# Keys turned on VectorE and by DMA, first states and the last block copies moved to ScalarE, in a gated delta rule layer with experts

## Chip, cores and metric

The kernel runs on one core of a Trainium2 chip, in one launch. The metric is device microseconds for the launch; lower is better. TensorE is called PE below, VectorE DVE, ScalarE ACT, GpSimd POOL and SyncE SP.

## What is computed

All tensors are float32, with 2 sequences of 512 tokens of width 256. The output is `x + delta_rule(xn) + ffn(xn)`, where `xn` is the layernorm of `x`. The second branch is attention with 16 heads, a shared expert and 16 routed experts with 4 picks per token. The first branch has 16 key heads and 32 value heads (R = 2 per key head), and takes most of the second half of the time:

```python
for each chunk:                      # the reference has chunks of 64 tokens, the kernel 128
    T  = solve(I + tril(beta * K K^T * decay, -1))     # T is the inverse
    vn = T @ (V * beta) - (T @ (K * beta * exp(g))) @ state
    out   = (Q * exp(g)) @ state + tril(Q K^T * decay) @ vn
    state = state * exp(g_last) + (K * exp(g_last - g))^T @ vn
x = out * silu(z); x = x * rsqrt(mean(x * x) + eps) * norm_weight
y += x @ W_out                       # per head
```

## The kernel before

Every engine has its own instruction stream, written out by hand in one function; semaphores (`fl["..."]`) are all that joins them. The order on an engine is the order of the calls in the code.

After the attention and the experts comes the part that the change touches: `for h in range(NK)` with NK = 16, on every engine. In pass h the scan of head h runs (two sequences b, four chunks m of 128 tokens), while head n = h + 1 is prepared (gates, values, triangular solve) and head f = h + 2 is begun (keys, queries, decays). PSUM is one tensor `ps` of 8 banks; X and Y are bank pairs 4, 5 and 6, 7.

What the text speaks of:

- PE's scan steps: `solved(h, m, b)` (L857) multiplies by the inverse PT; ACT's `deltas(h, m, b)` (L1440) takes the result to `vs`; `new_state(h, m, b)` (L867) multiplies the decayed, turned keys WT with it and waits for the deltas (`a_d`); `chunk_output` (L889, L890) follows; `key_state` (L843) multiplies the keys with the state; DVE's `residuals` (L2003) subtracts.
- DVE's `states(h, m, b)` (L2016 for m = 0, a copy; L2022 else) writes the state `St` from PSUM.
- `turn_keys(n)` (L797) transposes the 8 key tiles of head n on PE into the pair Y, and ACT's `decayed_keys(n, r)` (L1458) scales them into WT, 8 instructions for each r. It stands between `solved(h, 1, ·)` and `new_state(h, 1, ·)`.
- `project_gates` (L835) is filler between scan steps; PE's first one of a head waits for DVE's `system(n, ·)` (L1988), which writes MT and needs the decays that POOL's `scaled_decays` (L2373) finishes. `attention(n, r)` (L1996) writes AT.
- The inverse is built by doubling. `beside_64` and `blocks_of_128` are the last two steps; each takes two PSUM banks to SBUF, the first bank on ACT (L1503, L1507), the second on DVE (L2135, L2139).
- SP issues the DMAs: MT's diagonal blocks of 32 to DRAM (L392) and to `MTc` (L397, printed as front), back into `blk` (L404), then the decays of head f (L336). `T64c` holds turned blocks of the inverse.
- `add_experts(i)` (L2094) adds gathered expert rows: four instructions in each of the passes 0 to 7.

Of the kernel before, what the change touches and what calls it, by code (L numbers as in the profile page):

```python
# [45 lines left out]
def build(nc, d, out, debug=None):  # L46
# [9 lines left out]
    with ExitStack() as ctx:  # L56
# [200 lines left out]

        def stage_bank(f, i):
            return ((2, 0), (2, X))[f][i] if f < 2 else (X, Y)[i]
# [7 lines left out]
        def tiles(bank):  # L267
# [13 lines left out]
            "p_kq", "p_v", "p_z", "p_ss", "p_kk", "p_kt", "p_qk", "p_vt", "p_ks", "p_tr", "p_w", "p_o", "p_sx", "p_wo",  # L281
# [3 lines left out]
            "v_ck", "v_cv", "v_ss", "v_k2", "v_cb", "v_M", "v_A", "v_R", "v_S", "v_g", "v_sxt", "v_sx", "v_add",  # L285
            "v_base", "v_t0", "v_tt", "v_u3", "v_p3", "v_vs", "v_self",
# [13 lines left out]
        def _(sp):  # L300
# [86 lines left out]
            def blocks_out(n):  # L387

                sp.wait_ge(fl["v_M"], 2 * n + 2)
                for q in range(4):  # L390
                    rows = slice(q * BL, (q + 1) * BL)
                    dma(mt_dram[q].rearrange("u p c -> p u c"), MT[rows, :, rows]).then_inc(fl["d_m"], 16)  # L392
                if n:
# [75 lines left out]
            for s in range(SLOTS + 4):  # L469
# [6 lines left out]
                if s == SOLVE - 3:  # L476
                    blocks_in(0)
                if s == SOLVE + SB + 4:
# [44 lines left out]
        def _(pe):  # L523
# [268 lines left out]
            def turn_keys(n):  # L792
# [5 lines left out]
                last.then_inc(fl["p_kt"], 1)  # L798

            def project_values(n, r):  # L800
# [7 lines left out]
                elif r == 0:  # L808
                    pe.wait_ge(fl["a_wk"], 2 * n + 2)
# [30 lines left out]
            def key_state(h, m, b):  # L840

                pe.wait_ge(fl["v_S"], 6 * h + 2 * (m - 1) + b + 1)
# [3 lines left out]
            def solved(h, m, b):  # L846
# [3 lines left out]
                else:  # L850
# [3 lines left out]
                    pe.wait_ge(fl["a_p3"], h + 1)  # L854
                    pe.wait_ge(fl["v_p3"], h + 1)
# [169 lines left out]
            def second_beside_64_and_first_of_128(n):  # L1025

                pe.wait_ge(fl["a_u3"], n + 1)
# [9 lines left out]
            def second_of_128(n):  # L1037

                pe.wait_ge(fl["v_u3"], n + 1)
# [118 lines left out]
            for h in range(NK):  # L1158
# [28 lines left out]
                if middle:  # L1187
                    turn_keys(n)
# [77 lines left out]
        def _(act):  # L1266
# [170 lines left out]

            def deltas(h, m, b):
# [12 lines left out]
            def decayed_keys(n, r):  # L1451
                if r == 0:
                    act.wait_ge(fl["p_kt"], n + 1)
                    act.wait_ge(fl["v_cb"], n + 1)
                    if n >= 2:
                        act.wait_ge(fl["p_w"], 6 * (n - 1))
                for t in range(NT):
                    last = fn(WT[:, n % 2, r, t, :], tiles(Y)[:, t, :], ACT.Copy, scale=cb[:, r, 1, t:t + 1])  # L1458
# [42 lines left out]
            def beside_64(n):  # L1501
# [1058 lines left out]
```

## Time and profile before

| | |
|---|---|
| median of 3 runs | 1564.86 us (1560.41 to 1567.17) |
| profiled execution, its own time | 1548.47 us |
| its span, first to last instruction | 1546.7 us |
| granted TensorE clock, mean | 0.998 |
| PE / DVE / ACT / POOL busy | 98% / 71% / 50% / 29% |

The share of busy time is that of the whole span. Busy time of a run of matmuls on PE counts each until its modelled end, so the distance from one start to the next says what it costs.

### The profile page before, as it was taken

How to read it: one execution, taken by the hardware profiler on the slowest of the kernel's cores; microseconds unless marked ns; L12 is line 12 of the kernel's file. 1: busy time of each engine (PE TensorE's matmuls, PEld its weight loads, DVE VectorE, ACT ScalarE, POOL GpSimd, SP SyncE). 2: the span in 40 equal slices, each digit the busy share in tenths (PEclk: the TensorE clock that was granted, in tenths of full speed). 3: DMA queues.
4: the chain of work that ended last, by engine and by line, in shares of the span. 5: the costliest groups of instructions: out<-in, count | busy, mean ns of one | idle time of the engine just before them, and what ended most of it. 6: DMA issues, size and time to landing. Idle time of an engine off the chain costs nothing.

```text
span 1546.7 us, 29212 instructions
## 1 busy us (share of the span) xinstructions
PE 1514.5 (98%) x10946; PEld 1069.7 (69%) x10946; DVE 1104.5 (71%) x2452; ACT 779.7 (50%) x1680; POOL 442.7 (29%) x280
## 2 busy tenths in 40 slices
PE   6999999999999999999999999999999999999998
PEld 4666666767656776666767767767767668668667
DVE  5364544465366335698988988988888988988966
ACT  3444445344423334664564664664664565565552
POOL 1000000006024003354444444543442541541511
PEclk9999999999999999999999999999999999999999
DMA  4342433223144434324314414414313323223211
GB/s 135 99 150 96 156 124 109 66 64 125 54 128 130 124 109 120 94 51 97 100 35 107 107 32 108 105 36 106 78 50 91 70 60 86 69 66 86 60 22 35
DMA packets 225051, 136.88 MB, mean 89 GB/s; under 512 B 160976, under 2 KB 196304, under 8 KB 224912
## 3 DMA queue, kind: packets, MB, share of 16 engines
q1 hardware_dynamic: 221840, 126.62, 30.5%
q0 software_dynamic: 3072, 8.39, 1.8%
q8 instruction: 89, 1.46, 0.4%
q14 instruction: 50, 0.41, 0.1%
HBM read 94.85 MB, written 35.91 MB: 85 GB/s over the span
## 4 chain that ended last, share of the span: by engine, by line
PE 90%; DVE 3%; issue 2%; POOL 2%; ACT 1%; DMA 1%; SPq 0%; POOLq 0%; DVEq 0%; ACTq 0%
PE ps L953 7%; PE ps L814 7%; PE ps L575 7%; PE ps L835 6%; PE ps L670 5%; PE ps L600 4%; PE ps L1089 4%; PE ps L704 4%; PE ps L857 3%; PE ps L590 3%; PE ps L890 3%; PE ps L742 3%; PE ps L752 3%; PE ps L1112 3%; PE ps L867 3%; PE ps L889 2%
## 5 line engine op out<-in xcount | busy, mean ns | idle before, releaser
L1440 ACT ACTIVATE vs<-ps 128x256 f32<-128x256 f32 x128 | 49.2, 384 | 255.8 <-PE ps L857 251.6
L2389 POOL TENSOR_TENSOR qg<-qT,Ebc 128x1024 f32<-128x1024 f32 x32 | 74.7, 2354 | 354.4 <-PE ps L890 329.2
L1944 DVE SCALAR_TENSOR_TENSOR cv<-ps,cw,cv 128x1022 f32<-128x1022 f32 (+2 forms) x96 | 122.8, 1280 | 18.9 <-ACT cv L1380 14.9
L1955 DVE SCALAR_TENSOR_TENSOR cv<-ps,cw,cv 128x1022 f32<-128x1022 f32 (+2 forms) x96 | 122.6, 1277 | 4.0 <-ACT cv L1412 1.6
L835 PE MATMUL ps<-xnT,gz 128*128 128x512 f32 x256 | 121.0, 596 | 0.6 <-DVE cv L1944 0.6
L953 PE MATMUL ps<-wout,xT 128*128 128x256 f32 x480 | 120.2, 392 | 1.3 <-ACT vs L1427 0.9
L575 PE MATMUL ps<-xrT,cv 128*128 128x512 f32 x256 | 117.8, 593 | 1.1 <-ACT xrT L1277 0.8
L814 PE MATMUL ps<-xnT,gv 128*128 128x512 f32 x256 | 117.6, 603 | 0.5
L2083 DVE SCALAR_TENSOR_TENSOR total<-ps,rr,total 128x256 f32<-128x256 f32 x240 | 111.6, 481 | 5.7
L1340 ACT ACTIVATE we<-ps,bias 128x128 f32<-128x128 f32 (+3 forms) x128 | 65.8, 526 | 98.2 <-DVE bias L1764 98.2
L1760 DVE TENSOR_TENSOR ps<-ps,causal_neg 128x128 f32<-128x128 f32 x128 | 37.4, 292 | 105.2 <-PE ps L600 105.2
L953 PEld LDWEIGHTS ps<-wout,xT 128*128 128x128 f32 x480 | 86.1, 189 | 24.9 <-issue 11.7
L2373 POOL TENSOR_TENSOR dec<-dec,cb 128x1024 f32<-128x1024 f32 x32 | 60.0, 1897 | 147.5 <-DVE cb L1977 134.4
L814 PEld LDWEIGHTS ps<-xnT,gv 128*128 128x128 f32 x256 | 46.1, 189 | 71.0 <-issue 57.9
L890 PE MATMUL ps<-AT,vs 128*128 128x128 f32 x512 | 91.1, 275 | 0.0
L857 PEld LDWEIGHTS ps<-vs,PT 128*128 128x128 f32 x512 | 65.9, 191 | 24.1 <-issue 14.2
L2339 POOL TENSOR_SCALAR mean<-ssq 128x4 f32<-128x4 f32 x2 | 0.4, 192 | 284.9 <-ACT junk L1324 284.9
L1380 ACT ACTIVATE cv<-ps,cw 128x1024 f32<-128x1024 f32 x32 | 35.7, 1115 | 87.6 <-PE ps L752 61.1
L2359 POOL TENSOR_TENSOR dec<-dec,e_neg 128x1024 f32<-128x1024 f32 x32 | 75.2, 2373 | 0.0
L600 PE MATMUL ps<-front,we 128*128 128x128 f32 (+3 forms) x256 | 74.2, 433 | 0.8 <-ACT front L1283 0.8
L575 PEld LDWEIGHTS ps<-xrT,cv 128*128 128x128 f32 x256 | 46.1, 190 | 41.4 <-issue 39.4
L889 PE MATMUL ps<-qg,St 128*128 128x128 f32 x384 | 74.4, 275 | 0.0
(265 smaller groups left out, 3567.9 us busy)
## 6 DMA issues: line engine op xcount, KB each, us to landing
xs_dram<-zeros SPq DMA_DIRECT2D x16, 1024.0 KB, 7.6
dec<-grow_dram SPq DMA_DIRECT2D x32, 512.0 KB, 4.7
Ebc<-erow_dram SPq DMA_DIRECT2D x32, 512.0 KB, 5.0
cv<-in_wqk SPq DMA_DIRECT2D x16, 512.0 KB, 3.6
xn<-xs_dram SPq DMA_DIRECT2D x47, 128.0 KB, 2.1
ys_dram<-yg SPq DMA_DIRECT2D x47, 128.0 KB, 2.0
we<-in_we SPq DMA_DIRECT2D x16, 352.0 KB
cv<-in_wv SPq DMA_DIRECT2D x16, 256.0 KB, 3.7
```

Of the source, the lines that this page charges most:

```text
L575: last = mm(ps[:, 6 + j % 2, :], wqk[:, i, c, w * P:(w + 1) * P], xrT[:, c, at:at + S], start=(c == 0), stop=(c == HK - 1))
L600: mm(score(i, qt), aqT[:, q:q + P], akT[:, i * S:i * S + (qt + 1) * P], start=True, stop=True).then_inc(sm["s_sc"], 1)
L670: last = mm(ps[:, 6 + i, kt * P:S], vt[:, kt, i * P:(i + 1) * P], probT[:, 4 * i + kt, kt * P:S], start=(kt == 0), stop=(kt == 3), skip_gr ...
L814: last = mm(ps[:, (Y, X)[r] + b, :], gv[:, k, r * D:(r + 1) * D], xnT[:, k, b * S:(b + 1) * S], start=(k == 0), stop=(k == HK - 1))
L835: last = mm(ps[:, gate_bank(n) + b, :], gz[:, k, r * D:(r + 1) * D], xnT[:, k, b * S:(b + 1) * S], start=(k == 0), stop=(k == HK - 1))
L857: last = mm(ps[:, b, r * D:(r + 1) * D], PT[:, r * NT + 4 * b + m, :], vs[:, r, 4 * b + m, :], start=True, stop=True)
L889: mm(dst, St[:, m % 2, b * R + r, :], qg[:, r, t, :], start=True, stop=False)
L890: last = mm(dst, vs[:, r, t, :], AT[:, h % 2, r, t, :], start=(m == 0), stop=True)
L953: last = mm(ps[:, output_bank(h, t), r * H:(r + 1) * H], xT[:, r, t * P:(t + 1) * P], wout[:, r, :], start=True, stop=True)
L1944: ins = stt(row, pair(bank)[:, :, 0:S - k], cw[:, f, i, TAPS - 1 - k:TAPS - k], row, ALU.mult, ALU.add)
L1955: ins = stt(row, pair(bank)[:, :, 0:S - k], cw[:, n, 2 + r, TAPS - 1 - k:TAPS - k], row, ALU.mult, ALU.add)
L2083: ins = stt(total[:, t, :], ps[:, output_bank(h, t), r * H:(r + 1) * H], rr2[:, r, t:t + 1], total[:, t, :], ALU.mult, ALU.add)
```

## The change

- PE turns only head 0's keys. For n from 1 on DVE's new `turn_keys(n)` transposes the 32 x 32 blocks of all 8 tiles in one instruction (128 x 1024) from kT into T64c, and SP's new `keys_across(n)` carries the 16 blocks of the 4 x 4 grid to their places in WT, in 16 DMAs. ACT's `decayed_keys` scales from WT to WT, both after `gate_silu(n, 1)`.
- T64c loses its zeros by this, so POOL's new `empty_side(n)` clears a quarter of its rows and half of their columns when the DMAs have landed.
- DVE's copies of the first states go to ACT's `first_states`, and DVE's halves of the last two doubling steps go to ACT too.
- `add_experts(i, half)` adds two rows' tiles in each of the 16 passes, and the gathers are issued every second pass.
- SP issues the blocks back in before `MTc`, the keys behind them, and the decays of head f last.

```diff
+        turned_keys = T64c[:].rearrange("p u c -> p (u c)").rearrange("p (t n) -> p t n", t=NT)
+        def copies(n):
+            return 64 + (64 + 256) * n
@@ SP
+            def keys_across(n):
+                if n >= 2:
+                    sp.wait_ge(fl["p_w"], 6 * (n - 1))
+                sp.wait_ge(fl["x_kt"], n + 1)
+                for i in range(4):
+                    for j in range(4):
+                        src = turned_keys[i * BL:(i + 1) * BL, :, j * BL:(j + 1) * BL]
+                        dma(WT[j * BL:(j + 1) * BL, n % 2, 0, :, i * BL:(i + 1) * BL], src).then_inc(fl["d_c"], 16)
...
                     blocks_in(n)
+                    blocks_across(n)
+                    keys_across(n)
@@ PE
                     if f >= 2:
-                        pe.wait_ge(fl["a_wk"], 2 * f)
+                        pe.wait_ge(fl["v_A"], 2 * f)
...
-                pe.wait_ge(fl["d_c"], 64 * (n + 1))
+                pe.wait_ge(fl["d_c"], copies(n))
...
                         solved(h, 1, b)
-                if middle:
-                    turn_keys(n)
@@ ACT
+            def first_states(h, b):
+                act.wait_ge(fl["p_w"], 6 * h + b + 1)
+                if h:
+                    act.wait_ge(fl["p_o"], 8 * h)
+                fn(St[:, 1, b * R:(b + 1) * R, :].rearrange("p r d -> p (r d)"), ps[:, b, R * D:],
+                   ACT.Copy).then_inc(fl["x_S"], 1)
...
-            beside_64(0)
+            beside_64(0, 0)
+            beside_64(0, 1)
             gate_silu(0, 1)
             decays(1, 0)
             decays(1, 1)
-            blocks_of_128(0)
+            blocks_of_128(0, 0)
+            blocks_of_128(0, 1)
@@ DVE
+            def turn_keys(n):
+                dve.wait_ge(fl["p_u3"], 2 * n)
+                dve.transpose(turned_keys.rearrange("p t n -> p (t n)"), kT[:, n % 2].rearrange("p t n -> p (t n)"))                   .then_inc(fl["x_kt"], 1)
...
-                    for r in range(R):
-                        attention(n, r)
+                    attention(n, 0)
+                if middle:
+                    turn_keys(n)
                 if scan:
                     for b in range(B):
-                        states(h, 0, b)
+                        residuals(h, 1, b)
+                if middle:
+                    attention(n, 1)
@@ POOL
+            def empty_side(n):
+                pool.wait_ge(fl["d_c"], copies(n))
+                pool.memset(T64c[0:BL, :, BL:2 * BL], 0.0).then_inc(fl["g_zero"], 1)
```

PE's instructions from pass 0's second chunk, before (L857 `solved`, L797 `turn_keys`, L867 `new_state`, L889 `chunk_output`):

```order
L857 MATMUL ps<-vs,PT 128x128 [waits v_R]
L857 MATMUL ps<-vs,PT 128x128
L797 MATMUL ps<-ident,kT 128x128 [waits v_A]
L797 MATMUL ps<-ident,kT 128x128 x7
L867 MATMUL ps<-vs,WT 128x128 [waits a_d]
L867 MATMUL ps<-vs,WT 128x128
```

and of the changed kernel (L877 and L887 are `solved` and `new_state` there):

```order
L877 MATMUL ps<-vs,PT 128x128 [waits v_R]
L877 MATMUL ps<-vs,PT 128x128
L887 MATMUL ps<-vs,WT 128x128 [waits a_d]
L887 MATMUL ps<-vs,WT 128x128
L887 MATMUL ps<-vs,WT 128x128 [waits a_d]
```

Nothing stands any more between the product and the one that waits for its deltas.

SP's issues in pass 0, before:

```order
L392 DMA mt_dram<-MT 32x16x32 x3
L397 DMA front<-MT 32x16x32 [waits p_u1]
L397 DMA front<-MT 32x16x32 x3
L404 DMA front<-mt_dram 64x16x16 [waits d_m]
L404 DMA front<-mt_dram 64x16x16
L336 DMA dec<-grow_dram 128x1024 [waits v_A]
```

and of the changed kernel (L422 is `blocks_in`, L405 `blocks_across`, L415 `keys_across`):

```order
L422 DMA front<-mt_dram 64x16x16 [waits d_m]
L422 DMA front<-mt_dram 64x16x16
L405 DMA front<-MT 32x16x32 [waits p_u1]
L405 DMA front<-MT 32x16x32 x3
L415 DMA WT<-T64c 32x8x32 [waits x_kt]
L415 DMA WT<-T64c 32x8x32 x15
L341 DMA dec<-grow_dram 128x1024 [waits v_A]
```

Sixteen issues came in ahead of the decays, behind two sets that changed places.

ACT ahead of the loop, before (`beside_64`, `gate_silu(0, 1)`, `decays(1, ·)`, `blocks_of_128`):

```order
L1503 ACTIVATE U3s<-ps 64x512 [waits p_u3]
L1465 ACTIVATE sz<-ps 128x1024 [waits p_z]
L1469 ACT_TABLE_LOAD
L1469 ACTIVATE dec<-dec 128x1024 [waits g_mask] x2
L1507 ACTIVATE PT<-ps 64x8x64 [waits p_p3]
```

and of the changed kernel:

```order
L1531 ACTIVATE U3s<-ps 64x512 [waits p_u3] x2
L1493 ACTIVATE sz<-ps 128x1024 [waits p_z]
L1497 ACT_TABLE_LOAD
L1497 ACTIVATE dec<-dec 128x1024 [waits g_mask] x2
L1536 ACTIVATE PT<-ps 64x8x64 [waits p_p3] x2
```

The second of the two U3s copies waits for PE's second set of products there, and the decays of head 1 stand behind it.

## Rows read from the trace of the kernel before

**Rows 1.** Page, part 1: busy us (share of the span), instructions.

```profile
PE 1514.5 (98%) x10946; PEld 1069.7 (69%) x10946; DVE 1104.5 (71%) x2452; ACT 779.7 (50%) x1680; POOL 442.7 (29%) x280
```

**Rows 2.** Windows, two passes: length, busy of PE, PEld, DVE, ACT, POOL, PEclk, DMA.

```profile
706.25:765.21 58.96, 58.92 (x535) 42.28 (x534) 52.19 (x108) 33.87 (x64) 26.44 (x16) 1.00 0.34 81
1355.17:1414.12 58.95, 58.91 (x534) 42.27 (x533) 50.61 (x104) 33.86 (x64) 22.52 (x12) 1.00 0.32 74
```

**Rows 3.** Timeline of PE in one pass: start us, us, engine, line, operation.

```profile
941.32 1.05 PE L857 MATMUL ps<-vs,PT 128*128 128x128 f32 x8
942.21 1.04 PE L797 MATMUL ps<-ident,kT 128*128 128x128 f32 x8
943.09 1.06 PE L867 MATMUL ps<-vs,WT 128*128 128x128 f32 x8
...
958.83 0.38 PE L889 MATMUL ps<-qg,St 128*128 128x128 f32 x2
```

**Rows 4.** Timeline of PE in the last pass, which has no fillers.

```profile
1517.05 1.10 PE L857 MATMUL ps<-vs,PT 128*128 128x128 f32 x8
1518.17 1.16 PE L867 MATMUL ps<-vs,WT 128*128 128x128 f32 x8
1519.17 1.06 PE L890 MATMUL ps<-AT,vs 128*128 128x128 f32 x8
...
1521.36 1.23 PE L857 MATMUL ps<-vs,PT 128*128 128x128 f32 x8 [0.27 <-DVE vs L2003]
1522.54 1.23 PE L867 MATMUL ps<-vs,WT 128*128 128x128 f32 x8
1523.61 0.39 PE L889 MATMUL ps<-qg,St 128*128 128x128 f32 x2
```

**Rows 5.** Timeline of ACT in that pass; in brackets idle time before.

```profile
949.72 2.17 ACT L1458 ACTIVATE WT<-ps,cb 128x128 f32<-128x128 f32 x8
...
952.76 1.08 ACT L1465 ACTIVATE sz<-ps 128x1024 f32<-128x1024 f32 x1
956.86 0.83 ACT L1440 ACTIVATE vs<-ps 128x256 f32<-128x256 f32 x2 [3.02 <-PE ps L857]
```

**Rows 6.** Timeline of DVE in that pass.

```profile
933.81 1.21 DVE L1988 TENSOR_TENSOR MT<-ps,dec 128x1024 f32<-128x1024 f32 x1
...
938.11 0.75 DVE L2016 COPY St<-ps 128x256 f32<-128x256 f32 x2
```

**Rows 7.** Groups of DVE by form: busy, mean ns, idle before.

```profile
L2040 DVE STREAM_TRANSPOSE front<-ps 128x512 f32<-128x512 f32 x15 | 10.8, 717 | 1.5
```

**Rows 8.** Timeline of SP in that pass.

```profile
935.05 2.04 SPq L392 DMA_DIRECT2D mt_dram<-MT  x4
```

**Rows 9.** Two lines of SP: ns min/median/max of an issue, first and last start.

```profile
L397 SPq DMA_DIRECT2D front<-MT x64: 617/634/1827, 500.0 to 1469.9; - x64
...
DMA to landing us min/median/max: 2.2/2.4/4.0
```

**Rows 10.** The same for the 64 loads of 16 x 16 x 16.

```profile
L418 SPq DMA_DIRECT2D front<-tbt_dram x64: 303/448/474, 565.1 to 1495.0; - x64
```

**Rows 11.** Timeline ahead of the loop: PE, then ACT.

```profile
632.80 0.22 PE L1007 MATMUL ps<-T64c,MT 64*64 64x64 f32 x1
...
630.14 0.59 ACT L1503 ACTIVATE U3s<-ps 64x512 f32<-64x512 f32 x1
630.76 1.02 ACT L1465 ACTIVATE sz<-ps 128x1024 f32<-128x1024 f32 x1
...
633.09 2.00 ACT L1469 ACTIVATE dec<-dec 128x1024 f32<-128x1024 f32 x2
```

**Rows 12.** Timeline of pass 0: POOL, then DVE, then PE.

```profile
634.29 3.75 POOL L2373 TENSOR_TENSOR dec<-dec,cb 128x1024 f32<-128x1024 f32 x2 [13.11 <-ACT dec L1469]
...
638.08 1.23 DVE L1988 TENSOR_TENSOR MT<-ps,dec 128x1024 f32<-128x1024 f32 x1
...
639.71 1.88 PE L835 MATMUL ps<-xnT,gz 128*128 128x512 f32 x4
```

More of the change, by code:

```diff
@@ L477, in _ @@
                     blocks_in(0)
+                    blocks_across(0)
                 if s == SOLVE + SB + 4:
@@ L797, in turn_keys @@
                     last = pe.transpose(tiles(Y)[:, t, :], kT[:, n % 2, t, :], ident[:])
-                last.then_inc(fl["p_kt"], 1)
+                last.then_inc(fl["x_kt"], 1)
             def project_values(n, r):
@@ L1451, in decayed_keys @@
             def decayed_keys(n, r):
[L1452 to L1456, printed above, removed]
+                if n == 0:
+                    act.wait_ge(fl["x_kt"], 1)
+                else:
+                    act.wait_ge(fl["d_c"], copies(n))
+                act.wait_ge(fl["v_cb"], n + 1)
+                if n >= 2:
+                    act.wait_ge(fl["p_w"], 6 * (n - 1))
                 for t in range(NT):
-                    last = fn(WT[:, n % 2, r, t, :], tiles(Y)[:, t, :], ACT.Copy, scale=cb[:, r, 1, t:t + 1])
+                    src = WT[:, n % 2, 0, t, :] if n else tiles(Y)[:, t, :]
+                    last = fn(WT[:, n % 2, r, t, :], src, ACT.Copy, scale=cb[:, r, 1, t:t + 1])
                 last.then_inc(fl["a_wk"], 1)
@@ L1499, in blocks_of_64, with beside_64, blocks_of_128 @@
                    ACT.Copy).then_inc(fl["a_p2"], 1)
-            def beside_64(n):
-                act.wait_ge(fl["p_u3"], 2 * n + 1)
-                fn(U3s[64:P, 0:8], ps[64:P, 0, :].rearrange("p (u c) -> p u c", u=8), ACT.Copy).then_inc(fl["a_u3"], 1)
-            def blocks_of_128(n):
-                act.wait_ge(fl["p_p3"], 2 * n + 1)
-                fn(PT[0:64, 0:8, 64:P], ps[0:64, 0, :].rearrange("p (u c) -> p u c", u=8),
+            def beside_64(n, a):
+                act.wait_ge(fl["p_u3"], 2 * n + a + 1)
+                fn(U3s[64:P, 8 * a:8 * a + 8], ps[64:P, a, :].rearrange("p (u c) -> p u c", u=8),
+                   ACT.Copy).then_inc(fl["a_u3"], 1)
+            def blocks_of_128(n, a):
+                act.wait_ge(fl["p_p3"], 2 * n + a + 1)
+                fn(PT[0:64, 8 * a:8 * a + 8, 64:P], ps[0:64, a, :].rearrange("p (u c) -> p u c", u=8),
                    ACT.Copy).then_inc(fl["a_p3"], 1)
@@ L1589, in _ @@
                     for b in range(B):
+                        first_states(h, b)
+                    for b in range(B):
                         deltas(h, 1, b)
@@ L1596, in _ @@
                         deltas(h, 2, b)
-                if middle:
-                    decayed_keys(n, 1)
                 if scan:
@@ L1609, in _ @@
                     take_key(f, 0)
+                if ahead:
                     silu_key(f)
@@ L1645, in _ @@
                 if middle:
-                    beside_64(n)
+                    beside_64(n, 0)
                 if middle and not ahead:
@@ L1651, in _ @@
                 if middle:
-                    blocks_of_128(n)
+                    beside_64(n, 1)
+                    blocks_of_128(n, 0)
+                    blocks_of_128(n, 1)
         @block.vector
@@ L2087, in add_outputs, with add_experts @@
                     ins.then_inc(fl["v_add"], 1)
-            def add_experts(i):
-                for a in range(4):
+            def add_experts(i, half):
+                for a in range(2 * half, 2 * half + 2):
                     t, j = i % 2 * 4 + a, i // 2
@@ L2225, in _ @@
             second_values(0)
-            beside_64(0)
             for h in range(NK):
@@ L2233, in _ @@
                     system(n, 0)
-                if scan and middle:
-                    blocks_of_128(h)
                 if middle:
@@ L2240, in _ @@
                 if middle:
-                    for r in range(R):
-                        attention(n, r)
-                if scan:
-                    for b in range(B):
-                        states(h, 0, b)
+                    attention(n, 0)
+                if middle:
+                    turn_keys(n)
                 if scan:
@@ L2297, in _ @@
                     add_outputs(h, 4, 5)
-                    beside_64(n)
                     add_outputs(h, 5, 7)
@@ L2462, in _ @@
                 if middle:
+                    empty_side(n)
+                if middle:
                     if not ahead:
@@ L2476, in _ @@
                     key_norms(f)
-                if 0 <= n < 8:
-                    expert_rows(n)
+                if h % 2 and n // 2 < 8:
+                    expert_rows(n // 2)
 _OUT = (2, 512, 256)
```

58 lines of the change are left out of this document (23 added, 35 removed).

## The prediction

> **What bounds the kernel now.** I read the page's first part, then the windows of single passes, then the timelines of PE, ACT, DVE and SP around the places that the change touches. PE is busy 98% of the span [rows 1]. The windows run from the key turn of one pass to that of the next: 58.96 and 58.95 us, with PE busy 58.92 and 58.91 in them, while DVE has 52.19 and 50.61 and ACT 33.9 [rows 2]. The reader is to see two passes 650 us apart that have the same length to a hundredth: each pass costs exactly what PE has to issue, and nobody makes PE wait. Only 0.04 us are left. So what counts is what leaves PE's stream, and which wait comes up in its place. DVE has 6.8 us or more idle in a pass; relief for DVE is worth nothing by itself, and the 0.75 us for two state copies [rows 6] don't go to the time.
>
> **What is removed from PE.** The eight transposes start at 942.21 and the next group at 943.09 [rows 3], so they cost 0.88 us of PE's issue. They go in 15 passes (n = 1 to 15; head 0 stays): 13.2 us. I take the distance of starts and not the 1.04 us of the row, which reaches into the next group.
>
> **The wait that comes up.** The transposes covered something. `new_state(h, 1, 0)` needs ACT's deltas of `solved(h, 1, 0)`, and with the transposes gone both sequences' solves are all that stands between. The trace has this case: in the last pass no filler is left, and the solve is followed at once by the new state. Solve and new state together take 0.89 + 0.89 us when they don't wait (941.32 to 942.21 is one of them [rows 3]). In the last pass they take 1519.17 - 1517.05 = 2.12 us for m = 0 and 1523.61 - 1521.36 = 2.25 us for m = 1 [rows 4], so the pause is 0.34 or 0.47 us. In the second one the solve itself was still waiting for DVE's residuals; in the passes of the loop those lie under a filler, so the first is the nearer row and I take 0.34. What is left of the gain is 0.88 - 0.34 = 0.54 us a pass, times 15 = 8.1 us. Bounds: 0.41 x 15 = 6.2 us, and 13.2 us if ACT were quick enough for no pause at all, for which no row speaks.
>
> **What the ACT change costs ahead of the loop.** This is the part that I would overlook from the diff. `beside_64(0, 1)` stands ahead of `gate_silu(0, 1)` and the two decays of head 1 on ACT, and it waits for PE's second set of products. Those are issued until 632.80 + 0.22 = 633.0, while ACT's own first copy was done at 630.73 and the gate began at 630.76 [rows 11]. Now: second copy 633.1 to 633.7 (0.59), gate to 634.7 (1.02), table load to 636.0 (the 1.3 us between 631.78 and 633.09), so the decays start at 636.0 in place of 633.09, 2.9 us later. POOL's scaling followed the first of them: 634.29 becomes 637.2, and its two instructions (3.75 us) end at 641.0. DVE's second `system` starts right behind (638.08 before), takes about 1.15 us and ends at 642.2. PE's first gates of the pass started at 639.71 [rows 12] and wait for it: 2.5 us lost, once. PE then has nothing that gives them back, since it is the bound. Below, the cost is 2 us if parts overlap better; above, 3.5 us, since POOL's row gathers and the expert rows behind them come as much later as well, and `states(0, 1)` is queued behind those on DVE. Inside the loop the same move costs nothing: ACT's second U3s copy and the two PT copies lie under `key_products`, and DVE's copies did so before.
>
> **The keys' way round.** DVE: one transpose of 128 x 1024. The nearest rows are 0.717 us for 128 x 512 [rows 7] and 1.21 us for an operation of 128 x 1024 [rows 6]; 1.2 us, in a place from which two state copies (0.75) and one block copy went. DVE stays ahead of PE, cost 0. SP: `system(n, 1)` ended at 935.0 and SP began at 935.05 [rows 6, 8]; it is now about 1.2 us earlier, as two copies of the size of ACT's 0.59 us [rows 11] are gone from DVE ahead of it. From 933.85: 2.04 us for four issues [rows 8], some 1.7 for their landing (2.4 less an issue of 0.63 [rows 9]), two issues and then four at 0.63 with small gaps, 1.3 + 2.7: the keys' first issue is at 941.6. Sixteen issues follow. An issue took 0.634 us for 32 x 16 x 32 from SBUF to SBUF [rows 9] and 0.448 for 16 x 16 x 16, which is as many pieces as 32 x 8 x 32 has [rows 10]. So 7.2 to 10.1 us, and the last lands 1.8 us later: 950.6 to 953.5; I take 0.5 an issue, 951.4. ACT: the key scalings (2.17 us each [rows 5]) now both stand behind the second gate. It started at 952.76 with one scaling ahead of it; without that it waits for PE's gate products only and ends near 951.8. Then 4.3 us of scaling to 956.1, and `deltas(h, 3, ·)`, which began at 956.86 [rows 5], now 956.3 with PE ahead by 0.54. PE asks for the first of them at 958.83 - 0.54 = 958.3 [rows 3], and one takes 0.45: ACT may be 1.5 to 1.7 us late before PE loses anything, that is, the keys may land at 953.5. Even the upper bound just fits. Cost 0, with a cliff right behind it. If the cover is gone, every us of landing costs PE a us in 14 or 15 passes.
>
> The Trainium skill speaks against this part (VectorE: DVE Perf Modes, The three transpose paths): a plain DMA that transposes by strides is 19 times slower than the crossbar's transpose, which it puts at 1309 ns for 128 x 128 in bf16, and a full 128 x 128 turn belongs on TensorE. An estimate from that page would be 25 us a tile, and the keys would never be in time. Here DVE turns inside the blocks, and a DMA moves whole rows of 32 numbers; the four block transfers of MT are of that kind and land in 2.4 us [rows 9], so the sum goes by them.
>
> **Other edits at nothing.** The first states go from DVE to ACT, where ACT sat idle before the next deltas; DVE began at 938.11, ACT can begin with the products and be done before `key_state`. The split `add_experts` moves 2 of 4 additions from the early passes to the late ones, both with idle DVE. POOL's clearing lies in a wait for PE. `project_keys` waits for AT in place of WT, which is done sooner. `dec` is asked for some 10 us later on SP, and POOL uses it only behind the queries of the pass.
>
> **Sum.** -8.1 + 2.5 + 0.3 for small things in pass 0 = -5.3 us. The profiled execution took 1548.47 us (span 1546.7 and 1.8 around it), so it would become 1543.2. The median of the runs shown is 1564.86, 1.1% above that execution; I carry the difference over unchanged: 1559.5 us, 0.34% less. What a measurement of this kernel can tell from no change is about 0.5%, or 7.8 us.
>
> **Rivals.**
>
> - *The forecast*: PE stays the bound, a pass is 0.54 us shorter (58.41 us), 2.5 to 3 us lost at the start. 1557 to 1562. Chance 0.62.
> - *The gain stays nearly whole*: the pause after the solve is 0.1 to 0.2 us, or the start costs little, since POOL's and DVE's parts overlap. 15 x 0.73 - 2.5 = 8.5 us: 1556, and 1552 at the very best (13.2). For it: ACT is idle ahead of these deltas. Against it: ACT was idle in the last pass too, and the pause was there [rows 4]. Chance 0.19.
> - *The keys land late, and the time goes up*: one mechanism, SP's sixteen issues in a row. If an issue costs 0.70 in place of 0.5 us (L397 has single issues of 1.8 [rows 9]), they land at 954.6, 1.1 us past the point where ACT's deltas hold PE up; 14 passes x 1.1 = 15 us against 5.3 gained: 1575. It decides for slower than before from 0.655 us an issue on (0.38 us a pass). For it: no row has a DMA with both sides strided in SBUF, and no row has 26 issues in a run. Against it: the median of the larger transfer is 0.634. The page's rule on strided copies would end here too, far beyond. Chance 0.15.
> - *The change does nothing*: pause 0.47, start 3.5 us, ACT late in the last but one pass (it has no key projections between the fourth solve and its outputs, so the margin of 1.5 us is not there, about 1 us once): 6.2 - 3.5 - 1 = 1.7 us gained, 1563. Chance 0.04; it lies inside the range.
>
> **Range and chances.** From the middle of the second case to where the third has just begun: 1554 to 1569. Faster by over 0.5% needs over 7.8 us, the second case: 0.19. Slower by over 0.5% needs the third with 0.94 us a pass and more, most of it: 0.14. Within 0.5%: 0.67.
>
> **What would show it.** In the windows a pass of 58.4 us with PE busy some 0.3 less than that, and DVE still with idle time. In PE's timeline the new-state group (L887) starts 1.1 to 1.2 us after the solve for m = 1, with a wait for ACT. Ahead of the loop PE's first gates of pass 0 wait 2.5 us for DVE. On SP sixteen issues of 0.45 to 0.6 us, and ACT's scaling without a wait for DMA. The prediction is wrong if ACT waits for the keys until past 953.5 in the clock of rows 5 and PE then waits for ACT ahead of the outputs of m = 3, or if the pause after the solve is not there.

## The result and the profile after

The changed kernel takes 1592.36 us (median of 4 runs, 1584.41 to 1600.95), and the kernel before, measured beside it, 1562.63 us (4 runs, 1557.25 to 1567.17). The ratio is 1.019, 95% interval 1.012 to 1.0265: slower, outside the predicted range, on the side of the third rival. The profiled execution took 1597.63 us, span 1595.8.

The page of the changed kernel, part 1, for [rows 1]:

```profile
PE 1519.4 (95%) x10826; PEld 1065.4 (67%) x10826; DVE 1098.1 (69%) x2403; ACT 816.6 (51%) x1744; POOL 450.5 (28%) x295
```

PE's share fell from 98% to 95%: it has 120 instructions less and yet a longer span. Windows of four passes, from `key_products` (now L801) to the next, with the columns of [rows 2]:

```profile
650.22:717.56 67.34, 61.58 (x524) 43.65 (x524) 47.82 (x97) 39.57 (x70) 28.87 (x19) 0.95 0.31 67
717.56:777.74 60.18, 58.32 (x528) 41.33 (x524) 50.65 (x104) 36.18 (x67) 23.05 (x15) 1.00 0.35 80
1143.02:1203.61 60.59, 58.43 (x528) 41.24 (x525) 50.68 (x104) 36.17 (x67) 26.96 (x19) 1.00 0.38 88
1203.61:1263.60 59.99, 58.33 (x529) 41.33 (x525) 50.65 (x104) 36.19 (x67) 23.04 (x15) 1.00 0.35 80
```

A pass is no longer the same each time (59.2 to 67.3 us, against 58.95 to 59.5), and 1.7 to 2.2 us lie between its length and PE's busy time (5.8 in the first pass), where there was 0.04. So PE waits. The view of waits, largest sum us, times, longest us, says for what:

```profile
ACT WT L1486 <- DMA WT<-T64c: 51.1, 15, 4.8
...
PE ps L909 <- ACT vs L1465: 28.2, 15, 5.4
```

L1486 is ACT's `decayed_keys`, L1465 its `deltas`, L909 PE's `chunk_output`. Once in each of 15 passes ACT waits for the keys' DMAs, and once PE waits for ACT. The pass at 1143.02 shows how the one makes the other. SP's timeline, for [rows 8]:

```profile
1147.49 2.06 SPq L397 DMA_DIRECT2D mt_dram<-MT  x4
1152.18 1.35 SPq L422 DMA_DIRECT2D front<-mt_dram  x2
1153.57 2.69 SPq L405 DMA_DIRECT2D front<-MT  x4
1156.36 11.28 SPq L415 DMA_DIRECT2D WT<-T64c  x16
```

Then the timelines of ACT and PE in the same stretch, for [rows 5] and [rows 3]:

```profile
1162.13 0.83 ACT L1465 ACTIVATE vs<-ps 128x256 f32<-128x256 f32 x2 [3.28 <-PE ps L877]
...
1164.30 1.02 ACT L1493 ACTIVATE sz<-ps 128x1024 f32<-128x1024 f32 x1 [0.30 <-PE ps L856]
1168.94 4.78 ACT L1486 ACTIVATE WT<-WT,cb 128x128 f32<-128x128 f32 x16 [3.62 <-DMA WT<-T64c]
1173.63 0.63 ACT L1465 ACTIVATE vs<-ps 128x256 f32<-128x256 f32 x2
...
1169.36 1.05 PE L877 MATMUL ps<-vs,PT 128*128 128x128 f32 x8
1170.25 1.88 PE L763 MATMUL ps<-xnT,gkq 128*128 128x512 f32 x4
1174.05 0.49 PE L909 MATMUL ps<-qg,St 128*128 128x128 f32 x2 [1.91 <-ACT vs L1465]
```

The sixteen issues take 11.28 us and the last one lands with the start of ACT's scaling at 1168.94. ACT runs in order: the deltas of m = 3, whose products PE had done by 1170.4, stand behind the scaling, the first of them ends at 1174.0, and PE, which has worked off all its fillers by 1172.1, waits 1.91 us. The line of the keys' DMAs by itself (ns min/median/max of an issue; us to landing):

```profile
L415 SPq DMA_DIRECT2D WT<-T64c x240: 585/611/1848, 667.8 to 1528.9; - x120
...
DMA to landing us min/median/max: 1.9/2.0/3.3
```

**Where the time went.** From the first `key_products` of the loop to its last one, which is passes 0 to 13, the changed kernel needs 853.95 us and the kernel before 826.3: +27.65. The last two passes and what follows take 91.66 and 86.45: +5.2, with a wait of 5.44 us at the same place. Together 32.9 us, against a difference of the medians of 29.7. The profiled execution is longer still, since its loop starts at 650.22 and not at 633.90. That is not the change: those 16.3 us arise in the first stage, whose code is the same. There DVE stood still for 7 us in front of a copy while POOL issued its scatters of rows (`xs_dram`), and then took 9.36 us for four small operations (1.27 us in the profile before), beside two of POOL's (371.54 to 376.2):

```profile
369.00 0.69 DVE L1777 COPY front<-ps 128x512 f32<-128x512 f32 x1 [7.05 <-issue]
...
371.21 9.36 DVE L1933 TENSOR_SCALAR we<-we,prec 128x128 f32<-128x128 f32 x4
```

The loop starts at 632.9 to 633.9 in the profiles of e4 and e7 to e16, which have the same first stage, and at 641 to 651 in those of e1, e3, e5 and e6; e5 has the first stage of the kernel before, and its loop starts at 646.8. The kernel before, measured beside each of them, took 1561.98 us beside e1, e3, e5 and e6 and 1548.89 to 1551.01 beside the others. So times are compared by their ratio to it, and everything else below is read from the loop.

### The profile page after: what moved, and what is told of

Its sections match the earlier page's. It is cut to its first block, busy times and chain, and to the rows that moved or that the text cites. A ratio compares the mean times of both kernels' runs of the same rounds, so it can differ in the third digit from the quotient of the medians.

```text
span 1595.8 us, 29241 instructions
## 1 busy us (share of the span) xinstructions
PE 1519.4 (95%) x10826; PEld 1065.4 (67%) x10826; DVE 1098.1 (69%) x2403; ACT 816.6 (51%) x1744; POOL 450.5 (28%) x295
## 4 chain that ended last, share of the span: by engine, by line
PE 67%; SPq 12%; DVE 8%; ACT 6%; issue 3%; DMA 3%; POOL 0%; another core or an unknown queue 0%; POOLq 0%; ACTq 0%; DVEq 0%
SPq L415 9%; PE ps L973 7%; PE ps L596 7%; ACT WT L1486 4%; PE ps L691 4%; PE ps L835 4%; PE ps L621 4%; DVE cv L1979 4%; PE ps L1109 4%; PE ps L725 3%; PE ps L773 3%; PE ps L611 3%; PE ps L1132 3%; PE ps L679 2%; PE ps L1027 2%
## 5 line engine op out<-in xcount | busy, mean ns | idle before, releaser
L835 PE MATMUL ps<-xnT,gv 128*128 128x512 f32 x256 | 117.9, 604 | 3.3 <-DVE cv L1979 3.3
L1465 ACT ACTIVATE vs<-ps 128x256 f32<-128x256 f32 x128 | 47.0, 379 | 140.9 <-PE ps L877 134.2
L909 PE MATMUL ps<-qg,St 128*128 128x128 f32 x384 | 79.3, 290 | 28.3 <-ACT vs L1465 28.2
L1486 ACT ACTIVATE WT<-WT,cb 128x128 f32<-128x128 f32 x240 | 71.7, 388 | 51.1 <-DMA WT<-T64c 51.1
L910 PE MATMUL ps<-AT,vs 128*128 128x128 f32 x512 | 94.8, 283 | 0.0
L835 PEld LDWEIGHTS ps<-xnT,gv 128*128 128x128 f32 x256 | 46.8, 191 | 71.0 <-issue 54.9
L909 PEld LDWEIGHTS ps<-qg,St 128*128 128x128 f32 x384 | 61.2, 201 | 40.2 <-ACT vs L1465 40.2
L2043 DVE SCALAR_TENSOR_TENSOR vs<-ps,gates,vs 128x128 f32<-128x128 f32 x192 | 54.2, 345 | 44.1 <-PE ps L864 42.8
L2405 POOL MEMSET T64c<- 32x512 f32 x15 | 7.7, 514 | 264.7 <-DMA WT<-T64c 264.7
L877 PEld LDWEIGHTS ps<-vs,PT 128*128 128x128 f32 x512 | 65.9, 191 | 23.8 <-issue 14.2
```

The source lines that it names most:

```text
L835: last = mm(ps[:, (Y, X)[r] + b, :], gv[:, k, r * D:(r + 1) * D], xnT[:, k, b * S:(b + 1) * S], start=(k == 0), stop=(k == HK - 1))
L909: mm(dst, St[:, m % 2, b * R + r, :], qg[:, r, t, :], start=True, stop=False)
L910: last = mm(dst, vs[:, r, t, :], AT[:, h % 2, r, t, :], start=(m == 0), stop=True)
L1486: last = fn(WT[:, n % 2, r, t, :], src, ACT.Copy, scale=cb[:, r, 1, t:t + 1])
```

## The experiments

The theory: SP's issue time makes the keys late, and ACT's order carries the lateness to PE. The first rival: ACT is overloaded by what was moved to it, whenever the keys come.

**e3: four DMAs in place of sixteen.** They carry the same bytes, but whole rows, so that WT doesn't hold the turned keys.

```diff
-                    for j in range(4):
-                        src = turned_keys[i * BL:(i + 1) * BL, :, j * BL:(j + 1) * BL]
-                        dma(WT[j * BL:(j + 1) * BL, n % 2, 0, :, i * BL:(i + 1) * BL], src)
+                    for j in (i,):
+                        src = turned_keys[i * BL:(i + 1) * BL]
+                        dma(WT[j * BL:(j + 1) * BL, n % 2, 0], src)
```

> The changed kernel, but the turned blocks go to WT in 4 DMAs of 32 x 8 x 128 in place of 16 of 32 x 8 x 32: the same bytes, a quarter of the issues, and the blocks off the diagonal don't change places, so WT is not the transpose. Theory (SP's sixteen issues in a row make the keys late, and ACT's deltas of the fourth chunk are queued behind them): the keys land some 7 us earlier, ACT's wait for them (51 us in total in the changed kernel) falls under 2 us, PE's wait ahead of the fourth chunk's outputs (28 us) under 3 us, the granted clock no longer dips in the loop, a pass is 58.5 to 58.7 us, and the whole takes about 30 us less than the changed kernel, some 3 us less than the one before. Rival (ACT itself has too much between the second gate and those deltas since the first states, block copies and both scalings are there): PE still waits 1 us or more a pass, less than 15 us are won.

Measured 1552.98 us, ratio 0.9945 (0.9924 to 0.9966). SP's part in one pass:

```profile
1133.48 2.49 SPq L415 DMA_DIRECT2D WT<-T64c  x4
```

The passes are 61.12 and then 58.30 to 58.41 us, and the wait ahead of L909 is gone up to the last pass but one, where 0.94 us are left. ACT does all it does in the changed kernel, so it isn't overloaded.

**e1: ACT's scaling behind the deltas.**

```diff
                     gate_silu(n, 1)
-                    decayed_keys(n, 1)
-                    decayed_keys(n, 0)
...
                         deltas(h, 3, b)
...
                     take_key(f, 1)
+                    decayed_keys(n, 1)
+                    decayed_keys(n, 0)
                     take_key(f, 0)
```

> The changed kernel with all 16 DMAs, but ACT scales the keys behind the fourth deltas and the take of head f's keys. Theory (the landing hurts only because ACT takes its queue in order): PE's wait ahead of the fourth outputs is gone, a pass is 58.4 to 58.7 us, the whole about 3 us below the kernel before. Rival (ACT overloaded): the wait shows up again at the convolutions, PE's projection of the values waits for DVE by 0.5 us a pass or more, and a pass stays above 59 us.

Measured 1561.43 us, ratio 0.9997 (0.9977 to 1.0017). The keys come as late as ever and PE doesn't wait for deltas any more; behind the first pass they take 58.75 to 58.87 us. ACT in one of them:

```profile
1142.84 0.83 ACT L1465 ACTIVATE vs<-ps 128x256 f32<-128x256 f32 x2 [4.68 <-PE ps L877]
1145.01 1.11 ACT L1398 ACTIVATE cv<-ps,cw 128x1024 f32<-128x1024 f32 x1 [1.34 <-PE ps L763]
1146.02 4.78 ACT L1486 ACTIVATE WT<-WT,cb 128x128 f32<-128x128 f32 x16
1150.71 1.09 ACT L1398 ACTIVATE cv<-ps,cw 128x1024 f32<-128x1024 f32 x1
```

The hole for the scaling is 4.1 us (from 1146.1 until PE has the next products at 1150.2), the scaling takes 4.78, so the next key comes late and PE waits 0.47 us for DVE's convolution behind it. A wait went, a smaller one came, at the place that the rival had named, and 3 us below the kernel before, as expected, it did not get.

**e6: the change with the keys turned on PE again** (the keys' part undone, the rest kept), and **e5: the kernel before without the turns** for n from 1 (ACT scales whatever lies in PSUM, so the keys are wrong). The edit of e5:

```diff
-                if middle:
-                    turn_keys(n)
...
-                    act.wait_ge(fl["p_kt"], n + 1)
+                    act.wait_ge(fl["v_A"], 2 * n + 2)
+                    act.wait_ge(fl["p_kt"], 1)
```

> The changed kernel with only the keys undone: PE turns them as before, ACT scales them from PSUM where it did; first states and block copies on ACT and the experts' rows in halves stay. Theory: the loss of the changed kernel is all in the keys' way, so this one is level with the kernel before but for 2.4 us ahead of the loop and at most 0.1 us a pass: +2 to +4 us, verdict same. Rival (the work moved to ACT is to blame): 10 us slower than before or more.

> The kernel before, with PE's key turns of heads 1 to 15 left out and nothing in their place: ACT scales what lies in PSUM, so the output is not the layer's. It measures what the turns cost on PE once the pause behind the solve comes up. Theory: 0.88 us less a pass, 0.29 us of pause, 0.59 x 15 = 9 us less than before, no clock dip. Rival (something else bounds a pass just behind PE): less than 5 us.

e6: 1565.41 us, ratio 1.0021 (1.0003 to 1.0038), passes of 58.88 to 59.02, 2.12 us lost at the start. All the slowness is in the keys' part, and the other edits together give next to nothing. e5: 1555.33 us, ratio 0.9954 (0.9935 to 0.9972), passes of 58.37 at the end: the turns are worth 0.6 us a pass and no more, since the pause after the solve takes the rest. Up to pass 7 they are worth less, with passes of 58.59 to 58.74: PE's first gates start 0.25 us later into a pass there. The whole is 6.7 us below the kernel before, and not the 9 expected. Why those gates start later wasn't tried.

**e4: half of the sixteen DMAs issued by POOL**, with a count of their own, and everything else as in the change.

```diff
+            def keys_across(n):          # POOL; SP keeps i = 0, 1
+                if n >= 2:
+                    pool.wait_ge(fl["p_w"], 6 * (n - 1))
+                pool.wait_ge(fl["x_kt"], n + 1)
+                for i in range(2, 4):
+                    for j in range(4):
...
+                        pool.dma_start(WT[...], src).then_inc(fl["d_w"], 16)
```

> The changed kernel with eight of the sixteen key DMAs issued by POOL, on a semaphore of their own, in the 20 us in which POOL waits for PE. Theory (one queue's issue time is what is late): the keys land some 5 us sooner, no wait of ACT for them, a pass 58.3 us, 1552 to 1555 us. Rival (the landing of many small transfers, not their issue, is the time): the wait of ACT falls by less than 2 us.

Measured 1544.36 us beside 1549.05, ratio 0.9965 (0.9955 to 0.9975). SP's part, then ACT's scaling, in the profile of e4:

```profile
1116.63 6.37 SPq L415 DMA_DIRECT2D WT<-T64c  x8
...
1125.24 4.77 ACT L1487 ACTIVATE WT<-WT,cb 128x128 f32<-128x128 f32 x16
1130.02 0.83 ACT L1465 ACTIVATE vs<-ps 128x256 f32<-128x256 f32 x2
```

Five us of issue less, ACT doesn't wait, and thirteen passes are 58.30 or 58.31 us. This is the forecast's mechanism, with its ratio: 1559.5 / 1564.86 = 0.9966.

**e8: the keys ahead of `MTc` on SP**, and **e9: e8 with two small edits.** One takes ACT's second `beside_64` of the start behind its silu and decays; the other cuts PE's gate projection in two, so that its second half covers the pause after the solve.

```diff
-                    blocks_across(n)
                     keys_across(n)
+                    blocks_across(n)
@@ e9 too, ACT ahead of the loop, and PE
             beside_64(0, 0)
-            beside_64(0, 1)
             gate_silu(0, 1)
             decays(1, 0)
             decays(1, 1)
+            beside_64(0, 1)
...
-                    project_gates(n, 0, 1)
+                    project_gates(n, 0, 1, (0,))
...
                         solved(h, 1, b)
+                    project_gates(n, 0, 1, (1,))
```

> The changed kernel with two lines of SP's order exchanged: the keys' sixteen DMAs go ahead of the four that copy MT's blocks, which are needed later. Theory (a dose of lateness): the keys land 2.8 us sooner; ACT's wait for them falls from 3.4 us a pass to 0.3 to 1, PE's wait ahead of the fourth outputs from 1.9 us a pass to nothing or next to it, no clock dip in the loop, a pass 58.3 to 58.6 us, level with the run of four issues but for the last but one pass: 1553 to 1556 us. Rival (the number of small transfers, 240 more in all, disturbs other DMAs or ACT): a pass stays above 59.5 us.

> The keys-first order, and two more edits. Ahead of the loop ACT takes the second U3s copy behind the decays of head 1, as in the loop: PE's wait of 2.1 us for DVE's system and 0.25 us for PT in pass 0 are gone. And the gate product that stood ahead of the second chunk's solve is cut in two, one half ahead of it and one behind, to cover the pause of 0.29 us. Theory: a pass 58.0 to 58.1 us, 2.3 us less at the start, together 1548 to 1551 us, 0.8% below the kernel before. If the residuals are not ready half a gate product earlier, PE waits for DVE there and the second edit gives less.

Both missed: e8 1586.88 us, ratio 1.0239 (1.0217 to 1.0262); e9 1586.21, ratio 1.0228 (1.0198 to 1.0259). I had overlooked who counts what. One pass of e8, SP and ACT:

```profile
1138.91 11.08 SPq L415 DMA_DIRECT2D WT<-T64c  x16
1150.03 2.64 SPq L405 DMA_DIRECT2D front<-MT  x4
...
1154.35 4.78 ACT L1486 ACTIVATE WT<-WT,cb 128x128 f32<-128x128 f32 x16 [3.79 <-DMA front<-MT]
```

The keys' DMAs are issued by 1150, but ACT's releaser is now `front<-MT`: keys and `MTc` raise the same count `d_c`, ACT waits for all twenty, and their order among themselves gains nothing (PE's waits ahead of L909 come to 28.0 us in passes 0 to 13, against 22.8 in the changed kernel).

**e10: e8 with the keys on a count of their own**, and **e13: e10 with the two edits of e9.**

```diff
-                        dma(WT[j * BL:(j + 1) * BL, ...], src).then_inc(fl["d_c"], 16)
+                        dma(WT[j * BL:(j + 1) * BL, ...], src).then_inc(fl["d_w"], 16)
@@ ACT, and POOL likewise
-                    act.wait_ge(fl["d_c"], copies(n))
+                    act.wait_ge(fl["d_w"], 256 * n)
```

> Keys ahead of MTc's four transfers on SP, as in e8, and now with a count of their own (d_w), so that ScalarE's scaling waits for the sixteen key transfers alone; in e8 it waited for the count that MTc's transfers share (56.0 us over 15 passes, released by front<-MT). Theory (SP's issue time is what made the keys late; e8 missed because the shared count made ScalarE wait for all twenty): by e4's times SP would begin the keys at 1113.4 in the pass, end after 11.1 us at 1124.5, and they land 2.0 us later at 1126.5; ScalarE is free at 1125.2, its work then has about 1.5 us of slack ahead of chunk_output(h, 3), so it just fits: passes 58.3 to 58.7, no wait ahead of L909 over 0.3 us except in the last two passes, ratio to before 0.993 to 0.998. Rival (the order of the transfers doesn't matter, the keys' landing is late for another reason): as e8, passes 59 to 63, ratio 1.02. Second rival (MTc, now 11 us later, is the next late thing): a wait of PE in front of the blocks, and passes of 59 or more.

> e10 with the two small edits of e7 (ScalarE's second beside_64 of the start behind its silu and decays, so that the wait of 2.12 us at the start goes; the gate projection cut in two, its second half behind solved(h, 1)). Nothing is issued by GpSimd. Theory: e7's gains come on top: passes 58.0 to 58.4, no wait of PE at the start (the MT one), ratio to before 0.989 to 0.994. Rival: the keys are so close to their time that the shorter pass makes them late again: waits ahead of L909 and passes of 59 or more, ratio 1.00 or above.

e10: 1543.19 us beside 1548.89, ratio 0.9966 (0.9955 to 0.9977). Its pass, SP and ACT:

```profile
1114.35 11.25 SPq L415 DMA_DIRECT2D WT<-T64c  x16
...
1126.91 4.78 ACT L1486 ACTIVATE WT<-WT,cb 128x128 f32<-128x128 f32 x16 [0.85 <-DMA WT<-T64c]
```

The sixteen issues are as dear as before; they start one set of four earlier. ACT still waits 0.85 us, less than its slack, and eleven of the fourteen passes are 58.30 or 58.31 us. Two have a wait of PE of 0.89 and 1.04 us, where I expected none over 0.3: it fits by little. That the keys were late through SP and nothing else is shown by e3, e4 and e10, each in its own way.

**e7: e4 with the two small edits.**

> As the run with half of the DMAs on POOL, with the same two edits at the start and behind the solve. Theory: as the keys-first run with them, 1548 to 1551 us, and better than it only in the last but one pass, where the keys' landing still holds PE up: by 1 us at most.

e7: 1535.63 us beside 1549.05, ratio 0.9917 (0.9896 to 0.9938); e13: 1535.76 beside 1548.89, 0.9916 (0.99 to 0.9933). Passes of 58.01 or 58.02 us but for a few, which is 0.29 less than e4's, the pause of m = 1; the first pass is 57.98 in e7, against 61.12 in e4. Both beat both kernels. e13 needs no issue on POOL and is near its edge (a wait of 0.33 us in pass 0 and of 0.87 in another).

**e11, e12, e14, e16, e15: a wait of a chosen length.** Open was why some passes of the changed kernel cost 1.7 us more than their wait. e4 is the base; small activations ahead of ACT's scaling delay it.

```diff
+                if n and r:
+                    for i in range(15):          # 20, 25; 36 and 50 of 16 columns
+                        fn(idle[:, i], ident[:, 0:32], ACT.Copy)
                 for t in range(NT):
```

> e4 (no late keys, passes 58.30) with fifteen small activations (a constant copied to a buffer that nobody reads, 128x32, some 0.2 us each by the difference of a 128x128 and a 128x1024 one) ahead of ScalarE's scaling in each pass: a delay of about 3.1 us on ScalarE, of which 1.5 are slack, so a wait of about 1.5 us ahead of chunk_output(h, 3), short of 2.2. The output stays the reference's. Theory (waits up to 1.9 us cost themselves alone): passes of 58.3 + the wait = 59.5 to 60.2, granted clock 1.00 throughout the loop, ratio to before 1.005 to 1.014. Rival (any wait at this place lowers the clock): passes 1.7 us longer than 58.3 + wait.

> As e11, with twenty such activations: a delay of about 4.2 us and a wait of about 2.6 us, over the 2.2 us from which the passes of the changed kernel cost more than their wait. Theory (the granted clock falls after such a wait and costs some 1.7 us more): passes of 58.3 + 2.6 + 1.7 = 62.6 (62.0 to 63.2), clock under 1.00 in the stretch behind the wait, ratio to before 1.033 to 1.043. Rival (the lower clock in the changed kernel came from something else, as its transfers): passes 60.9, clock 1.00, ratio 1.02.

> As e11 and e12 (58.54 and 59.13 us a pass: a delay of 1.79 and 2.38 us, less a slack of 1.55, on top of 58.30), with 25 activations of 128x32. They delay ScalarE by 25 x 0.119 = 2.98 us, 1.43 more than the slack: passes of 59.7, a wait of 1.0 to 1.2 us in the records, clock 1.00. Both theories agree here; it is the point below.

> As e11, with 36 activations of 128x16 (0.10 to 0.12 us each, estimated from those of 128x32): a delay of 3.6 to 4.3 us, 2.1 to 2.8 over the slack, a wait of 1.8 to 2.5 in the records. Theory (a wait from 2.2 us lowers the granted clock, which costs some 1.7 us more): passes of 58.3 + excess = 60.4 to 61.1 if the wait is under 2.2, and 1.7 more if it is 2.2 or over. Rival (the clock fell for another reason): no addition at any wait.

> As e11, with 50 activations of 128x16: a delay of 5.0 to 6.0 us, 3.5 to 4.4 over the slack. Theory: the wait is over 2.2 us in every pass, the granted clock falls behind each, and a pass takes 58.3 + 3.5 to 4.4 + about 1.7 = 63.5 to 64.4. Rival (the clock fell for another reason): 61.8 to 62.7, clock 1.00.

e11 and e12 missed their dose: such an activation has a row of 0.217 us, but the next starts after 0.119 (0.20 and 0.106 for those of 16 columns). The table is read from the profiles, in us, behind pass 0. The delay is the distance from the first added activation to the scaling. The slack is e4's, where PE asks for the first delta at 1131.99 and ACT had it done at 1130.41, 1.58 us before; 1.55 is what fits e11, e12 and e14:

| run | delay | less 1.55 of slack | 58.30 + that | pass | wait of PE |
|---|---|---|---|---|---|
| e11 | 1.79 | 0.24 | 58.54 | 58.54 | under 0.3 |
| e12 | 2.39 | 0.84 | 59.14 | 59.13 | 0.56 |
| e14 | 2.98 | 1.43 | 59.73 | 59.73 | 1.16 |
| e16 | 3.80 | 2.25 | 60.55 | 60.55 or 62.2 | 1.98 |
| e15 | 5.28 | 3.73 | 62.03 | 64.85 | 3.46 |

Ratios: e11 0.999 (0.9981 to 1.0), e12 1.0047 (1.003 to 1.0063), e14 1.0094 (1.006 to 1.0128), e16 1.0251 (1.0218 to 1.0285), e15 1.0561 (1.0527 to 1.0596). Up to e14 lateness costs itself alone, to a hundredth. In e16 the same wait of 1.98 us is followed by two kinds of pass, seven of 62.2 us and six of 60.55, so my expectation of a fall from 2.2 us on was too high for these. Windows of PE behind the wait, first in a long pass, then in a short one (length, busy, PEclk, DMA):

```profile
1220.00:1225.00 5.00, 3.46 (x17) 0.72 0.24 49
...
1282.00:1287.00 5.00, 3.26 (x20) 1.00 0.23 48
```

and PE's timeline at the same two places:

```profile
1221.55 0.49 PE L910 MATMUL ps<-qg,St 128*128 128x128 f32 x2 [1.98 <-ACT vs L1466]
...
1223.24 0.64 PE L911 MATMUL ps<-AT,vs 128*128 128x128 f32 x2
1223.67 0.63 PE L910 MATMUL ps<-qg,St 128*128 128x128 f32 x2
...
1283.74 0.49 PE L910 MATMUL ps<-qg,St 128*128 128x128 f32 x2 [1.98 <-ACT vs L1466]
...
1284.96 0.39 PE L911 MATMUL ps<-AT,vs 128*128 128x128 f32 x2
1285.18 0.39 PE L910 MATMUL ps<-qg,St 128*128 128x128 f32 x2
```

Behind the one wait the pairs start 0.43 us apart, behind the other 0.22: PE runs at half its clock for a while, and the pass is 1.65 us longer (62.2 against 60.55). So the wait brings the clock down, not the transfers or the run: e4 has the same transfers and e14 the same kind of activations, and the clock of both is 1.00 throughout passes 1 to 13; e15's falls behind each of the waits, and costs 2.8 us a pass (1.7 in pass 1). The Trainium skill (TensorE: Matmul & The Clock Gate, Part 1: The HAM clock gate) gives this clock two states, 1.2 and 2.4 GHz, and says that activity lifts it to the upper one; the distances of 0.43 and 0.22 us agree.

The length of the wait alone doesn't decide it. PE's wait of 2.12 us at the start of pass 0 is followed by half the clock in eight of the twelve profiles that have it (e10's pass 0 takes 62.70 us, e4's 61.12), and in e9 a wait of 2.98 us was followed by the full clock, in a pass of 61.26 us, which is the 58.28 of its others plus the wait:

```profile
915.36 0.49 PE L909 MATMUL ps<-qg,St 128*128 128x128 f32 x2 [2.98 <-ACT vs L1467]
```

What else decides it is open.

## Why the prediction was wrong

**The step that failed** is "The keys' way round", which came out as "Cost 0, with a cliff right behind it". It was the right chain of events with wrong sizes, and the third rival describes what happened. From SP's start to ACT's scaling it took 17.55 us in the prediction (933.85 to 951.4) and 21.45 in the pass above (1147.49 to 1168.94):

- *Sixteen issues*: 8.0 us taken, 11.28 measured, +3.3, which is over the margin of 2.1 by itself. The row of one issue is 0.611 us, and 0.705 goes by from one to the next (10.4 to 11.8 us for the sixteen in the fifteen passes, 11.0 in the mean; 0.69 each). I had interpolated to 0.5 between a transfer from SBUF to SBUF and one from DRAM, as if the pieces set the price. They don't: 32 x 8 x 32 costs as much as 32 x 16 x 32 (0.634, [rows 9]), and e3's 32 rows of 4 KB cost 0.591. What makes 0.448 of the transfers in [rows 10] isn't separated: from DRAM as well, but for 64 x 16 x 16, an issue took 0.63 to 0.68. My upper bound of 10.1 us was a median of rows without the gap between them, so it was no bound.
- *The landing of the blocks that SP waits for*: 1.7 taken, 2.63 from the end of the fourth issue to 1152.18, +0.9; with the gaps in the sets before the keys +1.1.
- *The keys' own landing*: 1.3 us from the end of the last issue to the scaling, where I had 1.8: -0.5.
- *The scaling*: 4.3 taken, twice the 2.17 of [rows 5], 4.78 measured, +0.5. It reads SBUF now and no longer PSUM; that this is why wasn't tried.

The margin that I had worked out was right: keys at 953.5, or 2.1 us over the forecast. 3.9 + 0.5 - 2.1 = 2.3 us late, and the row gives 2.17 (the scaling starts at 1168.94; by e4 it could start 0.92 us behind the gate's start, at 1165.22; 1.55 of the rest is slack), of which 1.91 show as PE's wait. With the 0.27 us that come with each wait (0.22 of them ahead of L835) that is 2.18. By the rule of the table above, 58.30 plus what exceeds the slack, the pass would take 60.47 us; it takes 60.59, since PE's first gates start 0.11 us later into this pass than into the next.

**The sum for the loop.** 14 passes of 58.30 are 816.2 us. The waits ahead of L909 are 22.8 us in them and come with the 0.27 us each: 26.6. The start takes 2.4. What is left of 853.95 is 8.7, nearly all of it in four passes with waits of 2.18 to 3.08 us, whose matmuls run at half the clock afterwards, 1.65 to 1.8 us each and 3.3 in the first. In the third rival lateness was 1.1 us x 14 = 15, and the clock wasn't in the prediction at all. That it falls with PE's waits makes the cliff steeper by a third.

**The other steps.** *Turns and pause*: 0.88 - 0.34 = 0.54 us a pass predicted. In the changed kernel `solved`, `new_state` and `chunk_output` of m = 1 stand like this:

```profile
1155.05 1.05 PE L877 MATMUL ps<-vs,PT 128*128 128x128 f32 x8
1156.13 1.16 PE L887 MATMUL ps<-vs,WT 128*128 128x128 f32 x8
1157.12 0.39 PE L909 MATMUL ps<-qg,St 128*128 128x128 f32 x2
```

They make 2.07 us against 1.78 without a pause, so 0.29, and passes without a wait take 58.30 to 58.41 us in e3, e4 and e10 against the 58.41 predicted. Right. *The start*: 2.5 us predicted; PE's wait in the changed kernel is 2.12, with 0.25 at a place ahead of it (L877, for ACT's PT). Right, and e7 takes it away. ACT and PE there:

```profile
649.49 0.59 ACT L1531 ACTIVATE U3s<-ps 64x512 f32<-64x512 f32 x1 [2.44 <-PE ps L1027]
650.11 1.02 ACT L1493 ACTIVATE sz<-ps 128x1024 f32<-128x1024 f32 x1
651.15 1.28 ACT L1497 ACT_TABLE_LOAD   x1
652.44 2.00 ACT L1497 ACTIVATE dec<-dec 128x1024 f32<-128x1024 f32 x2
...
658.80 1.95 PE L856 MATMUL ps<-xnT,gz 128*128 128x512 f32 x4 [2.12 <-DVE MT L2023]
```

*DVE's transpose*: 1.2 us predicted, 1.24 measured (L2036), and in passes 1 to 13 PE waits for DVE only where it has waited for ACT before (0.22 us), in e4 nowhere. *The rule on strided DMAs* that I weighed, from the Trainium skill (VectorE: DVE Perf Modes, The three transpose paths), is given there for a large innermost stride at the destination, a condition that I had left out. It had no part in it: the keys' transfers land in 2.0 us. It was a question of how many, not of how strided. The page that would have helped is another one, the Trainium skill (DMA: Bandwidth & Descriptors, Rules for kernel authors): many small transfers are better made one large one, and under 64 KB one pays mostly overhead. Each of these has 32 KB, and the trace agrees as to the issue: 0.611 us for 32 KB and 0.634 for 64, and 2.5 us for the same bytes in four issues (e3) against 11.3.

**The chance.** The third rival had 0.15, decided from 0.655 us an issue on. What spoke for it stood in the prediction: "no row has 26 issues in a run". With a best guess of 8.0, a bound of 10.1 and a cliff at the bound, 0.15 was too low; and a range that ends at the cliff holds only if the cost does.

**Why the waits differ** (0.62 to 3.08 us in the changed kernel, while they are all alike in e11, e12 and e14 to e16). SP starts 4.47 us into every pass from 1 on, so a longer pass doesn't shift the next. What varies is behind that: the time until SP issues the blocks back in (3.5 to 5.2 us after its start) and single long issues in the run of sixteen. Three passes, which start at 1020.03, 1203.61 and 1323.24 and have waits of 2.61, 1.41 and 0.74 us:

```profile
1029.68 1.35 SPq L422 DMA_DIRECT2D front<-mt_dram  x2
1033.86 10.39 SPq L415 DMA_DIRECT2D WT<-T64c  x16
...
1211.60 1.35 SPq L422 DMA_DIRECT2D front<-mt_dram  x2
1215.82 11.80 SPq L415 DMA_DIRECT2D WT<-T64c  x16
...
1331.24 1.35 SPq L422 DMA_DIRECT2D front<-mt_dram  x2
1335.47 10.39 SPq L415 DMA_DIRECT2D WT<-T64c  x16
```

The second differs from the third by the run (+1.4 us, one issue of 1.72 in it), the first by the blocks (9.65 us into the pass in place of 8.00) and by a landing of 2.4 us behind the last issue in place of 1.3 in the others. In e4 and the five runs with added activations the keys are there before ACT asks for them, and none of it shows. Why an issue or a landing is long now and then is open, and so is what makes DVE stand still in the first stage in some executions only.

## What to carry to other kernels

- Price a run of DMAs by the distance from start to start, with the gap and the odd long issue, in a row of the same kind of memory on the same queue; from SBUF to SBUF the size of pieces hardly moved it here (0.59 to 0.63 us). Then add the landing that the queue itself waits for ahead of them.
- Work moved off the engine that bounds the kernel onto a queue is only free with slack. Work the slack out, as a time, ahead of the first in-order engine that waits; if the bound of the cost just fits, take the rival behind it as nearly as likely as the forecast.
- When transfers change places, look at the counts that the waits use: an earlier transfer on a shared count comes no earlier for who waits.

## What I had not expected of the hardware

- An issue on SP from SBUF to SBUF costs 0.61 us for 32 x 8 x 32 and 0.63 for 32 x 16 x 32, and in a run of sixteen one starts every 0.65 to 0.74 us, by the pass.
- Small activations overlap on ACT: a row of 0.217 us for 128 x 32, and one starts every 0.119 us.
- A wait of PE of 1.98 us (e16) lowered its clock in about half of the passes, 1.16 us (e14) never, 3.46 us (e15) always; it costs 1.65 us and, at 3.46, 2.8 us on top of the wait. The length alone doesn't decide it: in e9 one of 2.98 us did not lower it.
